# Engine loops for the projection steps, a later start for the scatter, and expert weights loaded in place, in a spiking attention and mixture-of-experts kernel

## What is computed

```
xn = (x - mean(x)) / sqrt(var(x) + eps)
Q, K, V = [layernorm(xn @ W.T + b, g, beta) >= 1.0 for W in (Wq, Wk, Wv)]   # 0 or 1
qk      = einsum('bhld,bhmd->bhlm', Q, K)                                   # 16 heads of 16
hamming = q_sum + k_sum.T - 2*qk
attn    = 16 - hamming + log_pe_bias(N, N)
out     = (attn * scale) @ V >= 0.5
attn_out = layernorm(out @ Wo.T + bo, go, betao) >= 1.0

logits  = xn @ router_w.T                 # 8 experts
gate    = top-2 of softmax(logits), scaled to sum 1
hidden  = silu(h[..., :256]) * h[..., 256:],  h = xn @ up_proj[e]
ffn_out = sum over the two experts of gate * (hidden @ down_proj[e])
x = x + attn_out + ffn_out
```

## Time and profile before

| what | value |
|---|---|
| median of 3 runs | 441.24 us (440.59 to 441.71) |
| span of the profiled execution | 510.6 us |
| PE busy in the span | 384.5 us (75%) |
| DVE, ACT, POOL busy | 273.3, 232.6, 211.0 us |
| mean granted TensorE clock | 0.883 of full speed |
| DMA | 58.98 MB, mean 116 GB/s |

### The profile page before, as it was taken

The page is one execution under the profiler, slowest core; times in us unless marked ns, Lnnn a source line. Parts: engine busy times, 40 slices in busy tenths (PEclk is TensorE's granted clock), DMA queues, the critical chain, the costliest instruction groups (busy, mean ns, idle before and its releaser), DMA issues.

```text
span 510.6 us, 9171 instructions
## 1 busy us (share of the span) xinstructions
PE 384.5 (75%) x2517; PEld 312.9 (61%) x2526; DVE 273.3 (54%) x774; ACT 232.6 (46%) x752; POOL 211.0 (41%) x213
## 2 busy tenths in 40 slices
PE   5498773110113999998999999999999999999960
PEld 2234662100112999997778888888888887667650
DVE  5799971000100687996545444554455442458995
ACT  1567421000001788986545544454445543366650
POOL 5242467777771000000233333333333333259993
PEclk9799985555555799999999999999999999999995
DMA  8721223222220111320443344343443332495222
GB/s 269 247 96 41 83 83 125 104 104 104 104 105 31 42 41 41 106 83 1 144 131 121 121 119 136 118 124 113 124 134 123 118 98 74 184 369 193 100 84 83
DMA packets 40432, 58.98 MB, mean 116 GB/s; under 512 B 6294, under 2 KB 27926, under 8 KB 40408
## 3 DMA queue, kind: packets, MB, share of 16 engines
q1 hardware_dynamic: 31712, 38.53, 24.5%
q0 software_dynamic: 6848, 18.70, 10.1%
q10 hardware_dynamic: 1848, 1.47, 0.9%
HBM read 35.79 MB, written 22.89 MB: 115 GB/s over the span
## 4 chain that ended last, share of the span: by engine, by line
PE 54%; issue 21%; DVE 10%; POOL 7%; DMA 3%; ACT 2%; SPq 1%; POOLq 0%; DVEq 0%; ACTq 0%
PE bank L1108 15%; PE bank L1109 14%; PE bank L1110 14%; POOL xres L718 3%; PE bank L1186 3%; PE bank L1251 3%; POOL xres L711 3%; PE bank L1235 3%; DMA xn<-x 2%; DVE xn L787 2%; DVE xst L765 2%; POOL rstd L703 1%; DVE w_f L808 1%; PE bank L1174 1%; PE bank L1195 1%
## 5 line engine op out<-in xcount | busy, mean ns | idle before, releaser
L692 POOL DMA_INDIRECT slot_y<-ey,dest x71 | 68.5, 965 | 214.6 <-ACT ey L554 186.2
L500 ACT ACTIVATE junk<-bank 128x256 bf16<-128x256 f32 x96 | 35.7, 379 | 89.8 <-remote 71.7
L677 POOL DMA_INDIRECT slot_x<-xn,pos x64 | 61.6, 963 | 23.9 <-issue 19.2
L996 DVE TENSOR_TENSOR hid<-gact,bank 128x256 f32<-128x256 f32 x71 | 29.9, 421 | 76.6 <-ACT gact L538 51.0
L1108 PE MATMUL bank<-ew,exT_h 128*128 x142 | 62.6, 441 | 5.6 <-issue 4.3
L1110 PE MATMUL bank<-w_h,xT_l 128*128 128x256 f32 x192 | 56.9, 296 | 11.3 <-issue 11.2
L795 DVE TENSOR_TENSOR xT_l<-xT,xT_h 128x256 fp32r<-128x256 f32 x28 | 12.9, 460 | 98.1 <-issue 54.1
L1109 PE MATMUL bank<-w_l,xT_h 128*128 128x256 f32 x192 | 56.9, 296 | 11.2 <-issue 11.2
L1108 PE MATMUL bank<-w_h,xT_h 128*128 128x256 f32 x192 | 57.1, 297 | 10.5 <-issue 10.4
L538 ACT ACTIVATE gact<-bank 128x256 f32<-128x256 f32 x71 | 27.4, 386 | 63.8 <-PE bank L1110 63.8
L1110 PE MATMUL bank<-ew,exT_l 128*128 x142 | 55.9, 394 | 0.0
(11 more groups left out here) (193 smaller groups left out, 967.9 us busy)
## 6 DMA issues: line engine op xcount, KB each, us to landing
ex<-slot_x SPq DMA_DIRECT2D x71, 129.0 KB
y_tok<-slot_y SPq DMA_DIRECT2D x8, 1024.0 KB, 13.6
ew_f<-experts SPq DMA_DIRECT2D x24, 256.0 KB, 2.6
xres<-x SPq DMA_DIRECT2D x16, 256.0 KB, 2.8
out<-xres SPq DMA_DIRECT2D x16, 256.0 KB, 2.1
xn<-x SPq DMA_DIRECT2D x6, 512.0 KB, 11.7
slot_y<-ey,dest POOLq DMA_INDIRECT x71, 2.8
xn<-x SPq DMA_DIRECT2D x4, 256.0 KB, 3.8
```

The lines of the kernel that those rows point to most:

```text
L500: nc.scalar.activation(junk[:, i, :], proj_ps[r][i], ACT.Square, accum_out=ssq[:, r, i:i + 1]).then_inc(s["ssq_done"], 1)
L677: pool.indirect_dma_start(slot_x, bass.IndirectOffsetOnAxis(ap=pos[:, k, t:t + 1], axis=0), xn[:, t, :], None).then_inc(s["scattered"], 16)
L692: pool.indirect_dma_start(slot_y, bass.IndirectOffsetOnAxis(ap=dest[:, m % 4:m % 4 + 1], axis=0), ey[:, m % 4, :], None).then_inc(y_out[m ...
L996: v.tensor_tensor(hid[:, m % 2, :], gact[:, m % 2, :], h_ps[m % 2][:, F:2 * F], ALU.mult).then_inc(s["hid_done"], 1)
```

## The change

The steps 0 to 3 are written out, and the steps 4 to 27 are engine loops: on PE one of six rounds, on ACT and DVE two of three rounds each; 28 to 31 are written out. `rest_of_routing` moves ahead of DVE's step 4, `open_kv` on PE ahead of step 4. The raw pieces are loaded straight to the lower half of their own place (`ew_f` is now a view of `ew`), in four DMAs of 8, 10, 4 and 2 pieces; the places of the early tensors change to suit, and `xT` lies where the spikes of Q and V go later, chunk by chunk. ACT waits for a set of pieces ahead of the first use. POOL's scatter waits, besides for `placed`, for `spk_done` 12, the spikes of tiles 0 to 3. The semaphore `kv_done` starts at 2, and its waits count 2 more.

```
-            for t in range(8):
-                body(t, t, None)
-            with eng.Fori(0, LOOP // 4) as i:
-                for u in range(4):
-                    body(i * 4 + (8 + u), 8 + u, i)
...
+        def steps(eng, first, last, body):
+            with eng.Fori(0, (last - first) // ROUND) as i:
+                for u in range(ROUND):
+                    body(i * ROUND + (first + u), first + u, i)
...
+PEEL, ROUND = 4, 4
+PIECE_SETS = [(0, 8), (8, 18), (18, 22), (22, PIECES)]
+PIECE_ROUNDS = [(4, 16, 8), (16, 28, 14)]
+LAST_STEPS = 28
...
@@ SP
-            loop(sp, POOL_PIECES + 2, 2, lambda n, m: load_piece(n, m % 2), peel=4)
-            for n in range(POOL_PIECES + 2, PIECES):
-                sp.wait_ge(s["piece_l"], n - 1 - POOL_PIECES)
-                sp.dma_start(ew_f[:, n % 2, :], pieces[:, n]).then_inc(piece_in[n % 2], 16)
+            def load_pieces(c):
+                lo, hi = PIECE_SETS[c]
+                sp.dma_start(ew_f[:, lo:hi, 1, :], pieces[:, lo:hi, :]).then_inc(piece_in[c], 16)
+            load_pieces(0)
+            sp.wait_ge(s["routed"], 1)
+            sp.wait_ge(s["xn_done"], NT)
+            sp.wait_ge(s["w_parted"], KC)
+            sp.wait_ge(s["wo_parted"], 1)
+            sp.wait_ge(s["bias_set"], 1)
+            load_pieces(1)
+            sp.wait_ge(s["pads_placed"], 1)
+            load_pieces(2)
+            sp.wait_ge(s["pads_done"], 16 * PC)
+            load_pieces(3)
...
             sp.wait_ge(s["scattered"], 16 * TOPK * NT)
-            sp.wait_ge(s["pads_done"], 16 * PC)
-            sp.wait_ge(s["piece_l"], PIECES - POOL_PIECES)
...
@@ ACT
-                    piece_upper(g - 2, g - 2)
+                    if g == 2:
+                        act.wait_ge(piece_in[0], 16)
+                    piece_upper(g - 2)
...
-                if m == 11:
-                    act.wait_ge(s["bias_set"], 1)
-                    act.wait_ge(s["pads_done"], 16 * PC)
...
-            steps(act, project)
-            last_steps(project)
+            for t in range(PEEL):
+                project(t, t, None)
+            for r, (lo, hi, n) in enumerate(PIECE_ROUNDS):
+                act.wait_ge(piece_in[1 + r], 16)
+                steps(act, lo, hi, lambda t, m, i: project(t, m, i * 2 + (n + (m - lo) // 2) if m % 2 else None))
+            act.wait_ge(piece_in[3], 16)
+            for t in range(LAST_STEPS, NT):
+                project(t, t, LAST_PIECES + t - LAST_STEPS)
...
@@ POOL
             pool.wait_ge(s["placed"], 1)
+            pool.wait_ge(s["spk_done"], G3 * PEEL)
             for t in range(NT):
...
@@ DVE
-            def later_project(t, m, i):
-                if not early(t, 4):
-                    project(t, m, i)
-                if m == 4:
-                    rest_of_routing()
-
-            steps(dve, later_project)
-            last_steps(project)
+            rest_of_routing()
+            for lo, hi, n in PIECE_ROUNDS:
+                steps(dve, lo, hi, lambda t, m, i: project(t, m, i, i * 2 + (n + (m - lo) // 2) if m % 2 else None))
+            for t in range(LAST_STEPS, NT):
+                project(t, t, None, LAST_PIECES + t - LAST_STEPS)
...
@@ PE
-                if m == 4:
-                    open_kv()
...
-            steps(pe, project_and_sum)
-            last_steps(project_and_sum)
+            for t in range(PEEL):
+                project_and_sum(t, t, None)
+            open_kv()
+            steps(pe, PEEL, LAST_STEPS, project_and_sum)
+            for t in range(LAST_STEPS, NT):
+                project_and_sum(t, t, None)
```

More of the change, by code:

```diff
@@ L132, in spiking_moe, with piece_at @@
         ew = put("ew", [P, PIECES, 2, PW], F32R)
[L135 to L150, removed]
+        ew_f = place_in(r_w)("ew_f", [P, PIECES, 2, PW])
+        def piece_at(n):
+            return r_w + n * 2 * PW * 4
+        put = place_in(piece_at(WEIGHT_PIECE))
         w_f = put("w_f", [P, KC, G4 * D])
@@ L179, in spiking_moe @@
         rc = put("rc", [P, route_const.shape[1]])
-        r_a = max(ends[r_q], ends[r_v])
+        assert ends[piece_at(ROUTE_PIECE)] <= piece_at(PAD_PIECE)
+        put = place_in(piece_at(PAD_PIECE))
+        pad_rows = put("pad_rows", [P, PC, ROW])
+        w_rt = put("w_rt", [P, KC, E])
+        assert ends[piece_at(PAD_PIECE)] <= piece_at(PIECES)
+        put = place_in(r_w)
+        y_tok = put("y_tok", [P, NB, B, TOPK, D])
+        spk = put("spk", [P, NB, B, D])
+        r_v = ends[r_w]
+        xT = place_in(r_v)("xT", [P, KC, NT, P])
+        v_spk = place_in(r_v)("v_spk", [P, NB * B * D], BF16)
+        r_q = r_v + NT * P * 4
+        qT = place_in(r_q)("qT", [P, NT, KC * P], BF16)
+        r_a = ends[r_v]
         put = place_in(r_a)
@@ L184, in spiking_moe @@
         w_l = put("w_l", [P, KC, G3 * D], F32R)
-        r_e = r_a + 2 * KC * G3 * D * 4
-        ew_f = put("ew_f", [P, 2, PW])
+        r_e = ends[r_a]
         ex = place_in(r_e)("ex", [P, 4, ROW])
@@ L247, in spiking_moe @@
         x_in = [sem(f"x_in{c}") for c in range(len(X_CHUNKS))]
-        piece_in = [sem(f"piece_in{i}") for i in range(2)]
+        piece_in = [sem(f"piece_in{i}") for i in range(len(PIECE_SETS))]
         ex_in = [sem(f"ex_in{i}") for i in range(4)]
@@ L512, in project @@
                     keep_xh(t + 1, m + 1)
[L513 to L518 removed]
+                if n is not None:
+                    piece_upper(n)
                 if m == 0:
@@ L972, in project @@
                     spikes(t - 3, m - 3, 1)
-                late = late_piece(m, i)
-                if late:
-                    piece_lower(*late)
+                if n is not None:
+                    piece_lower(n)
             dve.wait_ge(s["w_parted"], KC)
@@ L1134, in logits @@
                     pe.wait_ge(s["logitsT_set"], g - 1)
-                n = RG if (g + 1) * RG <= XT_TILES else RG // 2
-                for t in range(0, RG, n):
-                    where, at = xT_part(g * RG + t)
-                    for c in range(KC):
-                        last = mm(lgT_ps[g % 2][0:E, t * P:(t + n) * P].rearrange("e (t k) -> e t k", k=P), w_rt[:, c, :],
-                                  where[:, at:at + n, c, :], start=(c == 0), stop=(c == KC - 1))
+                for c in range(KC):
+                    last = mm(lgT_ps[g % 2][0:E, :], w_rt[:, c, :], xT[:, c, g * RG:(g + 1) * RG, :].rearrange("p t k -> p (t k)"),
+                              start=(c == 0), stop=(c == KC - 1))
                 last.then_inc(s["logitsT"], 1)
```

97 lines of the change are left out of this document (34 added, 63 removed).

## The result

| | before | changed |
|---|---|---|
| median of the timed runs | 441.48 us (440.59 to 442.25, 4 runs) | 453.11 us (452.85 to 453.82, 4 runs) |
| span of the profiled execution | 510.6 us | 451.1 us |
| that execution's own time | not recorded | 452.85 us |

The ratio on record is 1.0299, with an interval of 1.0266 to 1.0332, which is 13.2 us. The medians of the runs listed here differ by less: 453.11 / 441.48 = 1.0263, or 11.6 us. The record doesn't say from which times its ratio was formed, so the cost is known as 11.6 to 13.2 us, and it is clear of noise either way. The forecast was 453.2 us, slower. The span went the other way by 59.5 us, as the prediction said it might: the trace of before holds a stall that the timed runs of this comparison don't, and the trace of after has none. Here a run's own time is 452.85 - 451.1 = 1.8 us above its span.

A forecast was written before the change was run, and what follows sets the result against it. The prediction took the scatter on POOL to bound a stall-free timed run; the hold's 10.0 us plus the first load's 2 us made 12.0, so 441.2 + 12.0 = 453.2 us, with a range of 442 to 457.

The forecast's parts named there:

- The bound: Stall-free timed run before: the scatter from 65.5 to 163 ends last, not the projections, which end at about 152.
- at least 69.4 us of this stall is not in a timed run: PE, ACT and DVE pauses beside the scatter: the profiled span of 510.6 us exceeds the 441.2 median by this much.
- The hold, +10.0 us: POOL's first scatter DMA waits for twelve spike groups, so it starts at 75.5 instead of 65.5.
- The first load, +2 us: Eight raw pieces in one DMA make ACT and POOL's last reciprocal root late by 0.7 to 3.5 us; middle taken.
- The pace, 1.267 us: Time per scatter DMA on POOL, from 71 DMAs starting between 65.5 and 154.2 in the trace before.
- The way from its last DMA to the first product, 7.9 us: From the scatter's last DMA, through landing, expert tile load, turn and split, to PE's first expert product.
- Around the span, 5.9 us: Part of the 441.2 us median before left outside the stall-free span of 435.3 us.
- The loops, 0: Steps in loops on PE, ACT, DVE: 0.22 us a turn moves only the projections' end, which the scatter covers.
- The transposed `xT`, the other loads: Router's last group and later weight loads: 0 us, the loads hidden with some 7 us to spare.
- A, faster: Scatter pace under 1.09 us in timed runs, projections really stalled, loops cure that: 431.7 us; chance 0.13.
- B, projections late as well: Under 5.9 us around the span, first expert product before later than 163.1 by real stall: 449.3 us; chance 0.2.
- C, no change: Pace near 1.09 us, or the spared stall cancels the hold's loss: 440 to 442.5 us; chance 0.05.

The follow-up runs named there:

- kernel with small sets: Changed kernel without the scatter's second wait, its first load of raw weights split into four (pieces 0, 1, 2-3, 4-7): 439.93 us against 439.62 for the kernel before.

## Why the prediction was right

**The bound: right, and the stall was read only half right.** The scatter ends last in a plain session, and the projections don't: they end at 150.4 in the changed kernel and at 147.7 in that with small sets, and PE then waits 25 and some 15 us. The kernel before, which alone has ACT's wait for the padding DMAs, has no plain trace. With the hold its projections end at 166.9; with the scatter 10 us earlier that gives, as an estimate, at most 157, where the prediction had 152. So its margin is smaller than the prediction had it, but what the hold costs shows that the scatter comes last there too. (Rows 1 show the clock at 0.5 in seven slices from 77 to 166 us, not in eight; nothing hangs on it.) The step "at least 69.4 us of this stall is not in a timed run" holds for the runs of the result. As a general statement it is wrong: in four sessions the timed runs of before take 512 us, and its trace fits them, 510.6 + 1.8 = 512.4. The recording did not add the stall, as the step implied; trace and times are of two kinds of session. What saved the number was that the sum was built for a run without the stall, and never took a gain from it. That the result fell in a plain session was luck: in a stalled one the hold alone costs 2.9 to 3.9 us, and not 10.

**The hold, +10.0 us: right.** Alone it costs 9.8 us, give or take 2, and by the difference of ratios 8.1 to 9.7. The order of work on DVE gave it: the start at 75.5 was predicted for the kernel before with the hold, and it was 75.6.

**The first load, +2 us: right in sign, mis-sized, and half wrong in its reason.** `pos` came 2.4 us later in the changed kernel and 3.0 later in the two runs without the hold (67.97 and 67.94 against 64.98); the timed cost is 3.4 us, at the upper end of the 0.7 to 3.5 given; with small sets it is 0.3. The part of this step that failed is that "the lower half on POOL, which stands ahead of it" is what makes the root late and the root what makes the front late: with the root moved ahead 0.3 us is gained, because ACT's wait delays `xT_h` and the biases too. Measured alone, hold and load give 9.8 + 3.4 = 13.2 us, where the sum had 12.0; that 453.2 came within 0.1 us of the median is partly luck.

**The pace, 1.267 us: too short.** It came from a trace in which DVE stood still, and the remark that POOL's DMA takes 956 to 961 ns whether the other engines are busy or not is wrong: beside DVE's subtractions it takes up to 1477. Beside a working DVE the pace is 1.31 to 1.34, so the scatter takes 3 to 5 us longer than the sum had it, after the change and, by the kernel with small sets, before it too. **The way from its last DMA to the first product, 7.9 us: too long.** It is 177.24 - 171.66 = 5.6 us: 1.5 until SP's load, 2.2 for the load (3.48 was taken from a later one), and the rest for the turn and split. **Around the span, 5.9 us: too long**; it is 1.8. These three stand on both sides of the difference and so nearly cancel in it: the first expert product was put at 163.1 and 175.1, and was at 164.4 (in the kernel with small sets, the nearest to a plain record of before) and 177.2.

**The loops, 0: right.** Written out, the kernel takes the same time, to some 2 us. At the first turn of its loop PE takes 88.02 - 85.19 = 2.83 us for a step that otherwise takes 2.70. The five turns cost 0.13, 0.19, 0.09, 0.29 and 0.20 us, where the written-out steps take 2.70 throughout. All of it lies under the scatter:

```profile
82.49 0.28 PE L1149 MATMUL bank<-id_b,qk_spk 128*128 128x128 bf16 x2
85.19 0.28 PE L1149 MATMUL bank<-id_b,qk_spk 128*128 128x128 bf16 x2
88.02 0.27 PE L1149 MATMUL bank<-id_b,qk_spk 128*128 128x128 bf16 x2
```

The rule of the Trainium skill that the prediction weighed (Runtime: NRT & Kernel Launch, Instruction fetch mechanics), by which a taken branch to a target outside the two pages at hand stalls for a fetch, can account for no more than this, 0.29 us a turn; whether what is there is a fetch, no run tells.

**The transposed `xT`, the other loads: 0, right in sum.** The kernel with small sets keeps them, with the loops, and equals the one before to within 1.5 us; no run takes them one by one.

**The rivals.** A, faster: it needed a pace under 1.09 us and loops that cure the stall. The pace is longer, not shorter, and the loops crawl as well where there is a stall. B, projections late as well: the term that it rested on, less than 5.9 us around a span, is true, but its conclusion is not; the hold alone costs its full 9.8 us. The missing 4 us are partly in the scatter (the first expert product 1.3 us later than put) and partly behind it (438.1 - 164.4 = 273.7 us to the end in the kernel with small sets, where 272.2 was taken from the stalled trace); about 1 us is left, the size of the difference between sessions. C, no change, had nothing to cancel the hold in a plain session (in a stalled one the hold costs only 2.9 to 3.9 us).

**What stays open.** Why PE, ACT and DVE crawl beside back-to-back indirect DMAs in some sessions and not in others. The runs exclude that loops would end it, and show that it grows with the scatter, begins some us after it and outlives it by 4 to 14 us. Whether it belongs to the chip or to something else of a session they don't tell.

## What to carry to other kernels

Before a stall in a trace is priced, set the trace's span against the timed runs: if they differ by more than the few us that lie around a span, trace and times are of two conditions, and only differences built from work that both have can be trusted. A wait put ahead of a serial chain of DMAs that releases the next stage costs its full length, however much it helps engines that the chain covers; find first which chain releases the next stage. And a load merged from many small ones makes its first consumer wait for the last byte: split off what is wanted early.

## What the runs showed of the hardware

- **Two conditions of one program.** 440 or 512 us for the same kernel, by session or by chip, with nothing between them. In the stalled one PE leaves up to 2.43 us between single products, or stands for 23 us, beside GpSimd's indirect DMAs and for 4 to 14 us after them, whether the steps are written out or turns of a loop.
- **A DVE subtraction lengthens GpSimd's DMA.** An indirect DMA of 0.96 us takes 1.47 where it starts with 0.63 us of a two-operand DVE instruction still to run, and 1.14 with 0.30 left. A subtraction that begins 0.05 us or more after the DMA lengthens nothing.
- **An idle DVE makes the scatter faster.** For that reason the pace is 1.26 to 1.28 us in stalled sessions and 1.31 to 1.34 in plain ones: the engine that is stalled no longer disturbs the one that seems to stall it.
